# An encoder block with two attentions on one core: the decision flag made ahead of the stage change, query units from split operands, and the sums of heads turned by two DMAs

## The chip, the core and the metric

The kernel runs on one core of one Trainium2 chip. The metric is the device time of one execution in microseconds (us). The kernel before takes 1455.71 us, the median of three runs (1455.01 to 1456.9).

## What is computed

One block routes a context into a state (a small cross attention and gates, with layer norms); the next, with which this change deals, is a transformer layer on 2048 rows of width 256 with 16 heads of 16 features, whose second attention looks at the 1601 rows of the context. Cut to what matters:

```python
h = _layernorm(x, ln1_g, ln1_b)
x = x + _mha(h, h, sa_wq, ...)          # self attention, 2048 keys
h = _layernorm(x, ln2_g, ln2_b)
x = x + _mha(h, context, ca_wq, ...)    # cross attention, 1601 keys
h = _layernorm(x, ln3_g, ln3_b)
x = x + gelu(h @ mlp_w1.T + mlp_b1) @ mlp_w2.T + mlp_b2

def _mha(...):
    scores = einsum('bhqd,bhkd->bhqk', q, k) * HD ** (-0.5)
    p = softmax(scores, axis=-1)
    o = einsum('bhqk,bhkd->bhqd', p, v)
    return o.reshape(b, -1, WIDTH) @ wo.T + bo
```

All of it is float32. Where the kernel wants a product at TensorE's faster float32r rate with float32 accuracy, it splits both operands into a high and a low part and makes three products.

## The kernel before, in words

**Stages.** The first 425 us (the routed context, and keys, queries and values of the self attention) are not touched. Then come four chunks of 512 query rows of self attention (stage a = 0), four chunks of cross attention (a = 1), and an end of some 47 us.

**A chunk** works through four groups of four heads, each over all key tiles of 128 keys: 16 tiles in the self stage (64 steps a chunk) and 13 in the cross stage (52 steps). In a step PE makes the scores of the four heads in two halves (`scores`, L1457), ACT takes the exponential of each half (L1008, one instruction over 1024 columns), and PE multiplies the step before by the values (`pv`, L1474), into PSUM bank 6, where a group's sum over keys builds up. PE may be three halves of scores ahead of ACT (`LOOK`).

**Heads and sums.** After a group's last `pv`, DVE copies bank 6 (`copy_heads`, L2139). PE's first `pv` of the next group waits for this copy (semaphore `heads`, L1470). Features and softmax sums of a head stand in alternating blocks of 16 partitions, so after every second group DVE gathers the features of both in ONF and the sums in SUMS. The sums have to move by 16 partitions to stand beside the features they divide. Before, PE does this: DVE splits SUMS into RECH and SUML (L2157, L2158), PE multiplies both by a permutation matrix into bank 7 (L1496, L1497), DVE copies that to REC (L2167), takes the reciprocal in two halves (L2174) and multiplies ONF (L2178, semaphore `normed`).

**Side work.** The remaining work of a chunk of rows is laid into the steps of the next chunk by tables: `REST`, `LAST_REST` and `divide_unit` in `events` say at which step which piece stands. PE, DVE and others walk the same table in the same order, each taking its own part, so the tables are the program order of both. Pieces: `y`, the output projection of 128 rows (4 a chunk; it waits for `normed`); `h`, the turned layer norm (2); `u`, the query projection for the cross stage (2 units); `n`, norms of the queries; `m` and `o`, the MLP (8 and 4, cross stage only). They share PSUM bank 7: each piece of PE waits until DVE has taken the one before (`bank7_taken`). The list of parts gives a step for each, so "u": [25, 28, 38, 41] is two units in two parts each.

**The flag.** Whether scores are bounded (then no exact maximum is needed) is decided on data: DVE and PE reduce the norms to one number (`decide`, L1379, L2093, L2094), each engine loads it and branches (`general`). For the first three cross chunks it is made after the last self chunk, between the stages. SP waits for PE's `decided` before it loads the last group's keys of the cross stage.

**SP's queue** issues nearly all loads, in program order, each after a wait: queries of the next chunk a group at a time when `scores` of that group are done (L555, L561); during the last self chunk the cross stage's keys (L598, after the scores of each group), queries and values (L605, after `pv` of groups 1 and 3); then W1 and W2 of the MLP (L665, L666). The lines on which the order hangs:

```python
for g in range(GROUPS):
    last = (CHUNKS - 1) * GROUPS * NKS[0] + (g + 1) * NKS[0]
    sp.wait_ge(A[0]["scores"], 2 * last)
    if g == GROUPS - 1:
        sp.wait_ge(A[1]["decided"], 1)
```

Of the kernel before, what the change touches and what calls it, by code (L numbers as in the profile page):

```python
# [65 lines left out]
PARTS_OF = {"y": 1, "h": 1, "u": 2, "n": 2, "m": 2, "o": 4, "flag": 1, "w1": 1}  # L66
REST = [
# [5 lines left out]
LAST_REST = {"y": [5, 7, 9, 11], "h": [16, 17], "u": [19, 19, 21, 21], "n": [30, 30], "flag": [36], "w1": [42, 45]}  # L73
HAT_STEP = (16, 13)
GELU_STEP = 36
LOOK = 3

# [54 lines left out]
def build(nc, ctx, d, out):  # L132
# [9 lines left out]
    spreadR = m.new("spreadR", [P, P], F32)  # L142
# [35 lines left out]
    assert (TILES - LT) * HEADS * 32 * 4 >= HID * 4 + CHUNK * 4  # L178
    HCH = [m.put("HCH0", [P, CHUNK], F32, oV + LT * HEADS * 32 * 4 + HID * 4), m.new("HCH1", [P, CHUNK], F32)]
    HCL = m.put("HCL", [P, 2, CHUNK], F32, oXH + TPC * D * 4)  # L180
    W1L = m.put("W1L", [P, 2, HID], F32, oW1)
    RECH = m.put("RECH", [P, CHUNK], F32, oREC)
    SUML = m.put("SUML", [P, CHUNK], F32, oON + GP * CHUNK * 4)
# [6 lines left out]
    CAWQ = s.new("CAWQ", [P, 2, D], F32)  # L190
# [102 lines left out]
    def sm(o, n=1, p=P):  # L293
# [5 lines left out]
        saw_loaded w1_loaded w1_split w2_loaded v_cleared half_bias dve_chain dve_stepped  # L299
# [12 lines left out]
    only_cross = ("gelu", "mlp", "out_ready", "hc_lo")  # L312
# [117 lines left out]
    def events(a, first):  # L430
# [22 lines left out]
        if a == 1 or not first:  # L453
# [4 lines left out]
            ev[HAT_STEP[a]].append((o, "hat", 0, 0, True))  # L458
        return ev
# [9 lines left out]
    def _(sp):  # L469
# [75 lines left out]

        for a in range(2):
# [10 lines left out]
            def load_shift(c, g, s_to):  # L557
                rows = sd[a][:, g * GH:(g + 1) * GH, bass.ds(c * CHUNK, CHUNK)] \
                    .rearrange("r (j two) n -> two r j n", two=2)
                for odd in range(2):  # L560
                    sp.dma_start(QST[odd * HALF + SROW:odd * HALF + NROW, 2 * g:2 * g + 2, :], rows[odd]) \  # L561
                        .then_inc(s_to, 16)

# [19 lines left out]
            else:  # L583
# [3 lines left out]
                for g in range(GROUPS):  # L587

                    last = (CHUNKS - 1) * GROUPS * NKS[0] + (g + 1) * NKS[0]
                    sp.wait_ge(A[0]["scores"], 2 * last)  # L590
                    if g == GROUPS - 1:
# [10 lines left out]
                    if g % 2:  # L602

                        sp.wait_ge(A[0]["pv"], last)
                        sp.dma_start(V[:, 0:LT, (g - 1) * GH:(g + 1) * GH, :],  # L605
                                     vd.rearrange("p (k h e) -> p k h e", k=LT, h=HEADS)
                                     [:, :, (g - 1) * GH:(g + 1) * GH, :]).then_inc(s_vst[g // 2], 16)
# [55 lines left out]
            else:  # L663
                sp.wait_ge(A[0]["pv"], HALVES // 2)
# [4 lines left out]
                sp.dma_start(WOP[:], d["cawo"].rearrange("(g p) n -> p g n", p=P)).then_inc(A[1]["wop"], 16)  # L669
                general(2)  # L670
# [3 lines left out]
            for c in range(1, CHUNKS):  # L674
                for g in range(GROUPS):
# [3 lines left out]
                    load_shift(c, g, s_qst[a][g])  # L679

# [365 lines left out]
    def _(pe):  # L1046
# [324 lines left out]
        for a in range(2):  # L1371
# [15 lines left out]
            def general(f):  # L1387

                n_chunks = DECIDES[f][2]
                pe.wait_ge(at["flag"], decision(f)[2])  # L1390
                bounded = pe.value_load(flag[0:1, f:f + 1], min_val=0, max_val=1)
# [39 lines left out]

            decide(a)
            general(a)

            def scores(c, n, first):
# [26 lines left out]
            def pv(c, t):  # L1462
# [16 lines left out]
            def bank7_taken(c, kind, i, at=at):  # L1479

                q = c - 1
                s_, value = {"sums": (at["sums_taken"], c * GP + i // 2), "y": (at["y_taken"], q * TPC + i + 1),
# [3 lines left out]
                             "o": (at["mlp_taken"], q * TPC + i + 1),  # L1486
                             "flag": (A[1]["flag"], decision(2)[2])}[kind]
# [112 lines left out]
            if a == 0:  # L1600
                continue
# [779 lines left out]
```

## Time and profile before

| | us |
|---|---|
| median of three runs | 1455.71 (1455.01 to 1456.9) |
| the profiled execution's own time | 1458.83 |
| its span, first to last instruction | 1457.2 |
| PE / ACT / DVE busy | 1373.8 / 1086.6 / 590.9 |
| a self chunk, a cross chunk with MLP | about 123, about 128 |

How to read it: times in rows are us from the span's start unless ns is said. PE is TensorE's matmul, PEld its weight load, DVE VectorE, ACT ScalarE, POOL GpSimd, SP the queue that issues DMAs. In a timeline a row is: start, length, engine, line, operation, output <- input, count, and in brackets the idle time before it and what ended that. Matmuls overlap, so that the length of a row is a little more than the time to the start of the next piece. PEclk is TensorE's granted clock as a share of 2.4 GHz.

### The profile page before, as it was taken

The page shows a single profiled execution, that of the slowest core. Times are in us where ns is not written, and L with a number is a line of the kernel's source. Part 1 is how long each engine was busy: PE and PEld are TensorE (multiplying, and loading weights), DVE is VectorE, ACT ScalarE, POOL GpSimd, SP SyncE. Part 2 cuts the span into 40 slices and gives each one's busy share as a digit, 9 for nine tenths or more (in the row PEclk, how much of TensorE's full clock was granted, in tenths as well). Part 3 has the DMA queues.
Part 4 walks back from the last instruction along what each step waited for, and adds up shares of the span by engine and source line. Part 5 has one row for each costly group of instructions (what it writes and reads, how often), then busy time and mean ns, then how long its engine had stood idle before and what let it go on. Part 6 is the DMA issues. An engine that isn't in the chain of part 4 may idle for free.

```text
span 1457.2 us, 20715 instructions
## 1 busy us (share of the span) xinstructions
PE 1373.8 (94%) x8014; PEld 631.9 (43%) x8014; DVE 590.9 (41%) x1377; ACT 1086.6 (75%) x1357; POOL 47.5 (3%) x70
## 2 busy tenths in 40 slices
PE   7999989998779999999999999999999999999977
PEld 5667766786432223223322322332334333433437
DVE  5646676677740204313332331342441243144232
ACT  3543434455459999999999999799888788788843
POOL 2010000001010000000000000000000000000000
PEclk9999999999979999999999999999999999999998
DMA  9410001001268100000010353601000000000000
GB/s 306 164 47 1 1 0 58 1 1 53 72 164 119 31 23 13 27 27 14 12 52 14 46 107 62 158 30 37 24 12 16 23 12 12 23 15 1 5 11 15
DMA packets 35044, 66.00 MB, mean 45 GB/s; under 512 B 6202, under 2 KB 20092, under 8 KB 34204
## 3 DMA queue, kind: packets, MB, share of 16 engines
q1 hardware_dynamic: 29580, 43.24, 13.1%
q0 software_dynamic: 5360, 21.37, 4.1%
q8 instruction: 66, 1.08, 0.3%
q14 instruction: 38, 0.31, 0.1%
HBM read 42.70 MB, written 22.02 MB: 44 GB/s over the span
## 4 chain that ended last, share of the span: by engine, by line
PE 79%; ACT 10%; DVE 7%; issue 3%; DMA 0%; DVEq 0%; SPq 0%; ACTq 0%
PE PS L1474 27%; PE PS L1457 20%; ACT PX L1008 7%; PE PS L1556 2%; PE PS L1524 2%; PE PS L1244 2%; PE PS L1247 2%; PE PS L1206 2%; PE PS L1257 2%; PE PS L1207 2%; PE PS L1208 1%; PE PS L1505 1%; PE PS L1071 1%; PE PS L1539 1%; PE PS L1507 1%
## 5 line engine op out<-in xcount | busy, mean ns | idle before, releaser
L1008 ACT ACTIVATE PX<-PS 128x1024 f32<-128x1024 f32 (+1 forms) x928 | 869.9, 1108 | 99.8 <-PE PS L1457 77.5
L1474 PE MATMUL PS<-PX,V 128*32 128x512 f32 (+1 forms) x3712 | 498.8, 609 | 5.5 <-ACT PX L1008 4.0
L1457 PE MATMUL PS<-QST,stack 50*128 50x512 f32 (+1 forms) x1856 | 375.5, 467 | 12.1 <-ACT PX L1008 7.2
L1457 PEld LDWEIGHTS PS<-QST,stack 50*128 50x128 f32 (+1 forms) x1856 | 155.1, 184 | 391.4 <-ACT PX L1008 354.2
L1474 PEld LDWEIGHTS PS<-PX,V 128*32 128x32 f32 (+1 forms) x3712 | 74.0, 108 | 153.5 <-issue 130.9
L2139 DVE COPY OT<-PS 128x512 f32<-128x512 f32 x32 | 22.1, 692 | 214.1 <-PE PS L1474 213.3
L836 ACT ACTIVATE PH<-PS 128x512 fp32r<-128x512 f32 (+1 forms) x52 | 31.2, 600 | 82.8 <-PE PS L1187 73.0
L2174 DVE RECIPROCAL REC<-REC 128x256 f32<-128x256 f32 x30 | 52.6, 1753 | 1.0
L1556 PE MATMUL PS<-W,HIDT 128*128 128x256 f32 x192 | 44.6, 385 | 4.6 <-ACT HIDT L991 4.6
L854 ACT ACTIVATE TR<-PS,small 128x128 f32<-128x128 f32 x32 | 10.0, 364 | 51.2 <-PE PS L1247 51.2
L1866 DVE TENSOR_TENSOR PL<-PEXP,PH 128x512 fp32r<-128x512 f32 (+1 forms) x52 | 35.8, 689 | 28.0 <-ACT PEXP L837 27.2
L2235 DVE TENSOR_TENSOR XH<-PS,rows 128x256 f32<-128x256 f32 x12 | 5.1, 425 | 100.2 <-PE PS L1556 100.2
L2230 DVE TENSOR_SCALAR HIDT<-PS,cols 128x512 f32<-128x512 f32 x24 | 18.0, 751 | 66.7 <-PE PS L1507 66.7
L1206 PE MATMUL PS<-PH,CN 128*128 128x512 f32 (+1 forms) x104 | 44.0, 423 | 0.9 <-DVE PL L1866 0.9
L2203 DVE TENSOR_TENSOR XH<-PS,rows 128x256 f32<-128x256 f32 x28 | 11.9, 424 | 78.8 <-PE PS L1524 78.8
L1556 PEld LDWEIGHTS PS<-W,HIDT 128*128 128x128 f32 x192 | 35.2, 190 | 19.5 <-issue 14.8
L1207 PE MATMUL PS<-PH,CN 128*128 128x512 f32 (+1 forms) x104 | 42.2, 406 | 0.0
L1208 PE MATMUL PS<-PL,CN 128*128 128x512 f32 (+1 forms) x104 | 42.0, 404 | 0.0
L1757 DVE TENSOR_REDUCE small<-PS 128x1 f32<-128x512 f32 x64 | 35.1, 570 | 10.5 <-PE PS L1088 9.7
L1505 PE MATMUL PS<-HCH,W1H 128*128 128x512 f32 (+1 forms) x80 | 31.5, 394 | 3.8 <-DVE HCL L2250 3.8
L1167 PE MATMUL PS<-hF,SAW 128*128 128x512 f32 x64 | 31.6, 638 | 3.6 <-DVE small L1845 2.7
L2222 DVE TENSOR_SCALAR PARTS<-PS,cols 128x512 f32<-128x512 f32 x8 | 6.0, 751 | 67.1 <-PE PS L1539 67.1
(220 smaller groups left out, 1565.7 us busy)
## 6 DMA issues: line engine op xcount, KB each, us to landing
QST<-q_parts SPq DMA_DIRECT2D x192, 64.0 KB
q_parts<-PARTS POOLq DMA_DIRECT2D x16, 512.0 KB, 3.6
stack<-k_parts SPq DMA_DIRECT2D x24, 200.1 KB, 6.8
stack<-k_parts SPq DMA_DIRECT2D x18, 256.0 KB
k_parts<-KPARTS POOLq DMA_DIRECT2D x8, 512.0 KB, 3.2
v_cross<-V POOLq DMA_DIRECT2D x1, 3328.0 KB, 12.1
V<-v_cross SPq DMA_DIRECT2D x2, 1664.0 KB, 13.3
k_parts<-PARTS POOLq DMA_DIRECT2D x6, 512.0 KB, 3.3
```

The lines of the kernel that those rows point to most:

```text
L1008: act.activation(exp_place(a, h)[0:kr, :, :], PS[0:kr, slot:slot + 2, :], ACT.Exp, scale=SCALE).then_inc(at["exp"], 1)
L1167: ins = pe.matmul(PS[:, bank, :], SAW[:, "qk".index(kind), c, mm * P:(mm + 1) * P], hF[:, c, at:at + w], start=(c == 0), stop=(c == 1))
L1206: pe.matmul(PS[0:w, bank, :], c_hi, hi, start=first, stop=False)
L1207: pe.matmul(PS[0:w, bank, :], c_lo, hi, start=False, stop=False)
L1208: ins = pe.matmul(PS[0:w, bank, :], c_hi, lo, start=False, stop=last)
L1457: ins = pe.matmul(PS[0:kr, score_slot(a, h) + jj, :], KST[a][lo:lo + NROW, pair, kt * P:kt * P + kr].bitcast(F32R), QST[lo:lo + NROW, pair ...
L1474: ins = pe.matmul(PS[32 * j:32 * j + 32, 6, :], V[0:kr, kt, 2 * (g // 2 * GH + j) + g % 2, :], exp_place(a, 2 * (c * steps + t) + j // 2)[ ...
L1505: pe.matmul(out_, hi, h_hi, start=(c == 0), stop=False)
L1556: ins = pe.matmul(PS[:, 7, 0:D], HIDT[:, k, i * P:(i + 1) * P], W2[:, k, :], start=(k == 0), stop=(k == HID // P - 1))
L1757: ve.tensor_reduce(sm(MXP + tt * len(pcs) + p), PS[:, max_bank(m), 0:pcs[p][1]], AX, ALU.max) \
L1866: ve.tensor_tensor(PL[0:kr, n % RING, :].bitcast(F32R), PEXP[0:kr, n % RING, :], PH[0:kr, n % RING, :], ALU.subtract).then_inc(S["l0_lo"], 1)
L2174: ch(ve.reciprocal(part, part))
```

## The change

**Flag.** `decide(1)` becomes a piece at step 59 of the last self chunk, PE loads the flag at step 61, and the last `pv` of the self stage moves behind the first scores of the cross stage.

**Query units.** The activations HC (both stages) and the weights CAWQ (once, piece `wq` at step 20 of the first self chunk) are split; a unit is then six float32r products made in one step in place of four float32 instructions (a part of two in each of two steps). Steps of `y`, `u` and `n` change.

**Sums.** PE's two products, the split and the copy are gone. SP issues two DMAs (`turn_sums`) that bring SUMS, shifted by 16 partitions up and down, into REC and OT, and DVE puts the two together under masks (two instructions), at step 4 after the copy of the group instead of 2. The last pair of all keeps a product. In `copy_heads` the instruction on ONF now stands before the one on SUMS. The loads of values for groups 2 and 3 stand behind the cross stage's `general`.

```diff
-    {"y": [5, 8, 11, 14], "h": [19, 22], "u": [25, 28, 38, 41], "n": [54, 57]},
-    {"y": [5, 7, 9, 11], "h": [17, 18], "m": ...
+    {"y": [8, 10, 12, 14], "h": [19, 22], "u": [27, 27, 40, 40], "n": [54, 54]},
+    {"y": [8, 9, 10, 11], "h": [17, 18], "m": ...
-LAST_REST = {"y": [5, 7, 9, 11], "h": [16, 17], "u": [19, 19, 21, 21], "n": [30, 30], ...
+LAST_REST = {"y": [8, 9, 10, 11], "h": [16, 17], "u": [20, 20, 22, 22], "n": [30, 30], ...
+FIRST_REST = {"wq": [20]}
+FLAG_STEP, FLAG_LOAD = 59, 61
...
             if g % 2 == 0:
-                ev[t + 2].append((o, "sums", g, 0, True))
-                ev[t + 3].append((o, "divide", g, 0, False))
-                ev[t + 4].append((o, "divide", g, 1, True))
+                ev[t + 4].append((o, "sums", g, 0, True))
+                ev[t + 4].append((o, "divide", g, 0, False))
+                ev[t + 5].append((o, "divide", g, 1, True))
...
+        def turn_sums(a, u):
+            sp.wait_ge(A[a]["paired"], u)
+            sp.dma_start(REC[0:P - HD, :], SUMS[HD:P, :]).then_inc(A[a]["sums"], 16)
+            sp.dma_start(OT[HD:P, 1, :], SUMS[0:P - HD, :]).then_inc(A[a]["sums"], 16)
...
                     sp.wait_ge(A[0]["scores"], 2 * last)
+                    if g == GP:
+                        turn_sums(0, CHUNKS * GP - 1)
                     if g == GROUPS - 1:
                         sp.wait_ge(A[1]["decided"], 1)
...
-                    if g % 2:
...
+                    if g == 1:
+                        load_values(g, last)
...
             else:
-                sp.wait_ge(A[0]["pv"], HALVES // 2)
+                load_values(GROUPS - 1, HALVES // 2)
+                turn_sums(0, CHUNKS * GP)
                 sp.dma_start(W1[:], ...)
...
                     load_q(c, g, s_qst[a][g])
                     load_shift(c, g, s_qst[a][g])
+                    if g == GROUPS - 1:
+                        turn_sums(a, c * GP)
+                    if g == 1 and (a == 0 or c > 1):
+                        turn_sums(a, (c - 1) * GP + 1)
...
-                pe.matmul(PS[:, 7, :], spreadR[:].bitcast(F32R), RECH[:].bitcast(F32R), start=True, stop=False)
-                pe.matmul(PS[:, 7, :], spreadR[:].bitcast(F32R), SUML[:].bitcast(F32R), start=False, stop=True)
...
             def sums(c, g, at=at):
                 u = c * GP + g // 2
-                ve.wait_ge(at["sums"], u)
-                ve.tensor_copy(REC[:], PS[:, 7, :]).then_inc(at["sums_taken"], 1)
+                ve.wait_ge(at["sums"], 32 * u)
+                ch(ve.tensor_scalar(REC[:], REC[:], cols[:, LOWER:LOWER + 1], None, ALU.mult))
+                ch(ve.scalar_tensor_tensor(out=REC[:], in0=OT[:, 1, :], scalar=cols[:, UPPER:UPPER + 1], in1=REC[:],
+                                           op0=ALU.mult, op1=ALU.add))
```

**Order on the engines.** SP in the last self chunk, from the cross keys of group 1 to those of group 2. Before:

```order
L598 DMA stack<-k_parts 16x2x1601 [waits self_scores]
L598 DMA stack<-k_parts 16x2x1601 x5
L555 DMA QST<-q_parts 16x2x512 x6
L561 DMA QST<-shift 2x2x512 x2
L605 DMA V<-v_cross 128x13x256 [waits self_pv]
L598 DMA stack<-k_parts 16x2x1601 [waits self_scores]
L598 DMA stack<-k_parts 16x2x1601 x5
```

and with the change, where `REC<-SUMS` and `OT<-SUMS` are the two turning DMAs:

```order
L622 DMA stack<-k_parts 16x2x1601 [waits self_scores]
L622 DMA stack<-k_parts 16x2x1601 x5
L570 DMA QST<-q_parts 16x2x512 x6
L576 DMA QST<-shift 2x2x512 x2
L582 DMA V<-v_cross 128x13x256 [waits self_pv]
L558 DMA REC<-SUMS 112x512 [waits self_paired,self_scores]
L559 DMA OT<-SUMS 112x512
L622 DMA stack<-k_parts 16x2x1601 x6
```

The turn of the pair that DVE gathers at step 32 now stands behind the wait for the scores of group 2, ahead of its keys.

DVE in the same chunk, from that pair to the copy of group 2's heads (`COPY OT<-PS`), for which PE's next group waits. Before:

```order
L2157 CAST RECH<-SUMS 128x512 [waits dve_chain]
L2158 TENSOR_TENSOR SUML<-SUMS,RECH 128x512 [waits dve_chain]
L2160 SCALAR_TENSOR_TENSOR ONF<-OT,cols,ONF 128x512
L2167 COPY REC<-PS 128x512 [waits self_sums,dve_chain]
L2174 RECIPROCAL REC<-REC 128x256 [waits self_sums_taken]
L2174 RECIPROCAL REC<-REC 128x256 [waits dve_chain]
L2178 TENSOR_TENSOR ONF<-ONF,REC 128x512 [waits dve_chain]
L2222 TENSOR_SCALAR PARTS<-PS,cols 128x512 [waits parts_stored1,self_unit,self_normed]
L1696 TENSOR_TENSOR SQ<-PARTS 128x512 [waits self_unit_taken]
L1698 CAST PARTS<-PARTS 128x512 [waits squares]
L1699 TENSOR_TENSOR PARTS<-PARTS 128x512 [waits dve_chain]
L2139 COPY OT<-PS 128x512 [waits self_pv,parts_ready]
```

with the change:

```order
L2173 COPY OT<-PS 128x512 [waits self_pv,parts_ready]
L2184 SCALAR_TENSOR_TENSOR ONF<-OT,cols,ONF 128x512 [waits self_heads]
L2186 SCALAR_TENSOR_TENSOR SUMS<-OT,cols,SUMS 128x512 [waits dve_chain]
L2193 TENSOR_SCALAR REC<-REC,cols 128x512 [waits self_sums]
L2194 SCALAR_TENSOR_TENSOR REC<-OT,cols,REC 128x512 [waits dve_chain]
L2201 RECIPROCAL REC<-REC 128x256 [waits dve_chain] x2
L2205 TENSOR_TENSOR ONF<-ONF,REC 128x512 [waits dve_chain]
L2254 TENSOR_SCALAR PARTS<-PS,cols 128x512 [waits parts_stored1,self_unit,self_normed]
L1730 TENSOR_TENSOR SQ<-PARTS 128x512 [waits self_unit_taken]
L1732 CAST PARTS<-PARTS 128x512 [waits squares]
L1733 TENSOR_TENSOR PARTS<-PARTS 128x512 [waits dve_chain]
L2173 COPY OT<-PS 128x512 [waits self_pv,parts_ready]
```

The split and the copy from PSUM are gone; in their place two instructions on REC wait for `self_sums`, and behind them still stand the division, the query piece (`PARTS`, SQ) and the copy.

SP at the stage change. Before, from the last keys on:

```order
L598 DMA stack<-k_parts 16x2x1601 [waits cross_decided,self_scores]
L598 DMA stack<-k_parts 16x2x1601 x5
L555 DMA QST<-q_parts 16x2x512 x6
L561 DMA QST<-shift 2x2x512 x2
L605 DMA V<-v_cross 128x13x256 [waits self_pv]
L613 TENSOR_LOAD flag [waits cross_flag]
```

and with the change (the branch that is skipped left out):

```order
L622 DMA stack<-k_parts 16x2x1601 [waits cross_decided,self_scores]
L622 DMA stack<-k_parts 16x2x1601 x5
L570 DMA QST<-q_parts 16x2x512 x6
L576 DMA QST<-shift 2x2x512 x2
L633 TENSOR_LOAD flag [waits cross_flag]
...
L582 DMA V<-v_cross 128x13x256 [waits self_pv]
L558 DMA REC<-SUMS 112x512 [waits self_paired]
L559 DMA OT<-SUMS 112x512
L686 DMA W_70<-in_w1T 128x2x1024
L687 DMA W_71<-in_w2T 128x8x256
```

The values have moved behind the flag's load, and the turn of the last self pair stands behind them.

## Rows read from the trace of the kernel before

**Rows 1.** Stretches: length; busy PE, PEld, DVE, ACT, POOL; PEclk, DMA share, GB/s
```profile
548.00:671.00 123.00, 120.87 (x810) 36.78 (x806) 37.61 (x71) 118.31 (x128) 2.00 (x3) 1.00 0.08 24
1154.00:1282.00 128.00, 123.89 (x766) 49.10 (x766) 42.45 (x80) 106.38 (x110) 2.17 (x4) 1.00 0.06 18
```
**Rows 2.** Timeline of ACT, second self chunk: runs of exponentials and the idle time between
```profile
563.85 5.60 ACT L1008 ACTIVATE PX<-PS 128x1024 f32<-128x1024 f32 x6 [0.43 <-PE PS L1457]
569.89 5.61 ACT L1008 ACTIVATE PX<-PS 128x1024 f32<-128x1024 f32 x6 [0.43 <-PE PS L1457]
...
628.10 40.44 ACT L1008 ACTIVATE PX<-PS 128x1024 f32<-128x1024 f32 x44 [0.43 <-PE PS L1457]
```
**Rows 3.** Timeline of PE, same chunk: two steps with no piece between, and a query part
```profile
585.71 1.06 PE L1474 MATMUL PS<-PX,V 128*32 128x512 f32 x8
...
587.37 1.06 PE L1474 MATMUL PS<-PX,V 128*32 128x512 f32 x8
...
595.59 1.12 PE L1539 MATMUL PS<-HC,CAWQ 128*128 128x512 f32 x2
```
**Rows 4.** Timeline of PE, second cross chunk: an MLP unit of six products, then the sums' products
```profile
1084.02 0.50 PE L1505 MATMUL PS<-HCH,W1H 128*128 128x512 f32 x1
...
1085.61 0.74 PE L1457 MATMUL PS<-QST,stack 50*128 50x512 f32 x4
...
1087.27 0.51 PE L1496 MATMUL PS<-RECH,spreadR 128*128 128x512 f32 x1
...
1087.93 0.73 PE L1457 MATMUL PS<-QST,stack 50*128 50x512 f32 x4
```
**Rows 5.** Timeline of DVE, last self chunk: gathering, division, query piece, copy of the heads
```profile
856.80 0.75 DVE L2151 SCALAR_TENSOR_TENSOR SUMS<-OT,cols,SUMS 128x512 f32<-128x512 f32 x1
...
861.13 3.54 DVE L2174 RECIPROCAL REC<-REC 128x256 f32<-128x256 f32 x2
...
874.18 0.75 DVE L2222 TENSOR_SCALAR PARTS<-PS,cols 128x512 f32<-128x512 f32 x1 [8.78 <-PE PS L1539]
...
876.15 0.69 DVE L1699 TENSOR_TENSOR PARTS<-PARTS 128x512 fp32r<-128x512 f32 x1
...
886.42 0.69 DVE L2139 COPY OT<-PS 128x512 f32<-128x512 f32 x1 [9.58 <-PE PS L1474]
887.15 0.49 DVE L2148 TENSOR_SCALAR ONF<-OT,cols 128x512 f32<-128x512 f32 x1
```
**Rows 6.** Timeline of SP, last self chunk: keys of group 2
```profile
883.09 2.65 SPq L598 DMA_DIRECT2D stack<-k_parts  x6
```
**Rows 7.** DMA issues, 905 to 950 us (KB each, median us from issue to landing)
```profile
V<-v_cross SPq DMA_DIRECT2D x1, 1664.0 KB, 12.7
...
WOP<-in_cawo SPq DMA_DIRECT2D x1, 256.0 KB, 2.8
shift<-Rp POOLq DMA_DIRECT2D x1, 64.0 KB, 2.2
```
**Rows 8.** Timeline at the stage change: last self `pv` but one, SP's loads, first output projection
```profile
912.32 1.07 PE L1474 MATMUL PS<-PX,V 128*32 128x512 f32 x8
...
916.94 3.73 SPq L598 DMA_DIRECT2D stack<-k_parts  x6
...
924.13 0.54 SPq L605 DMA_DIRECT2D V<-v_cross  x1
...
930.68 1.13 PE L1524 MATMUL PS<-WOP,ONF 128*128 128x256 f32 x4
```
**Rows 9.** Busy time by stretches around both starts of a stage (columns as in rows 1)
```profile
431.00:432.00 1.00, 1.00 (x6) 0.20 (x8) 0.00 (x0) 1.00 (x2) 0.00 (x0) 0.50 1.05 123
...
923.00:924.00 1.00, 1.00 (x8) 0.23 (x10) 0.00 (x0) 1.00 (x2) 0.00 (x0) 0.57 1.11 135
...
930.00:935.00 5.00, 5.00 (x36) 1.59 (x28) 2.02 (x5) 4.38 (x6) 0.00 (x0) 1.00 1.10 341
```
**Rows 10.** Timeline at the end: the last product of the sums
```profile
1410.64 1.12 PE L1494 MATMUL PS<-SUMS,spread 128*128 128x512 f32 x2 [1.70 <-DVE SUMS L2151]
```

More of the change, by code:

```diff
@@ L458, in events @@
             ev[HAT_STEP[a]].append((o, "hat", 0, 0, True))
+        else:
+            for kind, at in FIRST_REST.items():
+                for t in at:
+                    ev[t].append((0, kind, 0, 0, True))
+        if a == 0 and c == CHUNKS - 1:
+            ev[FLAG_STEP].append((0, "flag", 0, 0, True))
         return ev
@@ L1430, in general, with scores @@
                     pe.sem_inc(at["decided"], 1)
-            decide(a)
-            general(a)
-            def scores(c, n, first):
+            if a == 0:
+                decide(0)
+                general(0, load_flag(0))
+            else:
+                general(1, bounded)
+            def scores(c, n, first, a=a, at=at, NK=NK, steps=steps):
                 h = c * steps * 2 + n
@@ L1492, in sums, with hidden @@
                 pe.wait_ge(at["paired"], c * GP + g // 2)
[L1493 to L1500 removed]
+                pe.matmul(PS[:, 7, :], spread[:], SUMS[:], start=True, stop=True).then_inc(at["sums_taken"], 1)
+            def hidden(kind, out_, i, c, span):
                 w = slice(i * P, (i + 1) * P)
[L1503 removed]
+                if kind == "u":
+                    hi, lo = CAWQH[:, c, w].bitcast(F32R), CAWQL[:, c, w].bitcast(F32R)
+                else:
+                    hi, lo = W1H[c][:, w].bitcast(F32R), W1L[:, c, w].bitcast(F32R)
                 h_hi, h_lo = HCH[c][:, span].bitcast(F32R), HCL[:, c, span].bitcast(F32R)
@@ L1533, in piece @@
                     ins.then_inc(at["hT"], 1)
-                if kind == "u":
-                    if first:
-                        pe.wait_ge(at["hc"], 2 * q + 2)
-                    for c in share(2):
-                        ins = pe.matmul(PS[:, 7, :], CAWQ[:, c, i * P:(i + 1) * P], HC[:, c, :],
-                                        start=(c == 0), stop=(c == 1))
-                    if last:
-                        ins.then_inc(at["unit"], 1)
-                if kind == "m":
+                if kind in "um":
+                    if kind == "u" and i == 0 and first:
+                        pe.wait_ge(S["wq_split"], 1)
                     if first:
@@ L1575, in chunk @@
                     for o, kind, i, part, last in ev[t]:
-                        if kind in ("copy", "divide", "hat", "w1"):
+                        if kind in ("copy", "sums", "divide", "hat", "w1", "wq"):
                             continue
@@ L1582, in chunk @@
                         held = (co, kind, i, A[o])
-                        if kind == "sums":
-                            sums(co, i, A[o])
-                        elif kind == "flag":
-                            decide(2)
+                        if kind == "flag":
+                            decide(2 if a == 1 else 1)
                         else:
@@ L2140, in copy_heads @@
                 ve.wait_ge(at["heads"], u + 1)
-                end = at is A[1] and c == CHUNKS
                 if g % 2:
```

130 lines of the change are left out of this document (66 added, 64 removed), and 2 rows, old and new, of the table REST.

## The prediction

> **What bounds the kernel now.** I read the stretches by stage first, then the timelines of ACT and PE inside a chunk, then DVE and SP around the places where the change puts a wait. In a self chunk ACT is busy for 118.3 of 123 us, in a cross chunk with MLP for 106.4 of 128 while PE has 123.9 [rows 1]. So self chunks go at ACT's pace and cross chunks at PE's. ACT makes 44 exponentials in 40.44 us, 0.916 us each if I leave out about 0.1 us of overlap at the end [rows 2]: a step of two takes 1.83 us. PE, when it is behind, starts its `pv` of one step at 585.71 and of the next at 587.37 [rows 3]: 1.66 us. PE's slack is thus 0.17 us a step, and a piece of side work is paid for by what it is longer than the slack gathered. Two output projections three steps apart show it: ACT's runs restart at 563.85 and 569.89, 6.04 us apart [rows 2], and 3 x 1.66 + 1.06 is 6.04. A projection part costs PE 1.06 us. With a full lead, ACT idles 0.43 us beside the overlap of 0.1 for such a part [rows 2], so the lead hides about 0.55 us of one piece.
>
> **The change part by part.** The sum is made against the profiled execution (span 1457.2, own time 1458.83), which is 3.1 us above the median of 1455.71; I add the difference to the median.
>
> *Sums without products.* A pair costs PE 0.66 us (1087.27 to 1087.93 [rows 4]). In self chunks (0.66 against a lead of 0.55) and at step 2 of cross chunks this stands in steps that go at ACT's pace, and is hidden: 0. The second pair of a cross chunk stands among MLP units, where PE is always behind: 0.66 in each of three chunks, **-2.0**; some 0.3 in the first cross chunk.
>
> *Query units.* Before, a unit is two parts, each as long in the queue as a projection part (records of 1.12 and 1.13 us [rows 3, 8]): 2.12 us. Six float32r products take 1.59 us (1084.02 to 1085.61 [rows 4]). PE saves 0.53 a unit, but in self chunks two parts use the lead twice and one piece once: 2 x (1.06 - 0.55) is 1.02, 1.59 - 0.55 is 1.04. So 0 in self chunks, and 2 x 0.53, **-1.1**, in the first cross chunk, where both parts of a unit already stood in one step. The split of HC gives DVE about 2.3 us a chunk (two casts, two subtractions), in 123 us of which it is busy for 38 [rows 1], ahead of a unit five steps later: 0.
>
> *Projections two steps apart or side by side.* In a self chunk the four are behind ACT by 4 x 1.06 - 6 x 0.17 - 0.55 = 2.7 us in place of about 2.5; in a cross chunk four parts take PE 10.9 us from step 8, and from step 5 to 11 they took it as long as it will now take ACT to reach step 8 and PE to do the rest. 0, with 1 us either way for all chunks.
>
> *The turned sums in an ordinary chunk.* From the copy of the heads to `paired` DVE takes 0.69 + 2 x 0.75 us [rows 5]; two DMAs and 2.2 to 2.8 us to land [rows 7] follow, then on DVE 0.49 + 0.75 for the two instructions, 3.54 for the reciprocals, 0.69 for the product [rows 5], 5.5 in all. That is some 11.5 us after the copy, and `y` stands at step 8, 14.6 us after: hidden by 3 us. SP's query loads ahead of it end before `paired`.
>
> *The turned sums in the last self chunk.* Here they aren't hidden. DVE gathers the pair at step 32 (856.80 [rows 5]) and wants it turned at step 36. But SP issues this turn only after the scores of group 2, where it issues keys at 883.09 before [rows 6]. Queued on DVE behind `self_sums`: 5.5 us of division, the second query piece with 2.56 (0.75 + 0.69 + 0.43 + 0.69, 874.18 to 876.84 [rows 5]), and then the copy of group 2's heads, without which PE can't begin `pv` of group 3. With 0.45 for two issues (2.65 for six [rows 6]) and 2.8 us to land as WOP, the row nearest in size (256 KB, against 224 each [rows 7]), the copy starts at 883.09 + 0.45 + 2.8 + 8.2 = 894.5 in place of 886.42 [rows 5]. PE and ACT stand still for **+8.0**. Bounds: 2.2 us to land gives 7.4, 4 us gives 9.2.
>
> *TensorE's clock after it.* At the stage change PE's work ends at 913.4 but for a last `pv`, the flag holds it up, and the clock is at 1.2 GHz until about 923.9 [rows 8, 9]; SP's load shows that PE got on at 916.9, so it was low for nearly 7 us of work. After the wait at the first stage's start it was still low at 431 to 432 [rows 9], some 7 us after its first scores. At half clock a step takes 3.32 us in place of 1.83, so 6.7 us cost 3.0: **+2.9**. Bounds: 0 if the clock stays, 3.6 if it is low for 8 us. The Trainium skill ("TensorE: Matmul & The Clock Gate", Terms) takes the penalty as the throttled time times (1 - K/N), at half clock half of it; by that the term would be 3.4 and the sum 0.5 more.
>
> *The stage change.* SP's loads of the last keys wait for `decided`, which comes at 916.94 now [rows 8], and with the flag made earlier when the last but one `pv` is through, at 912.32 + 1.07 = 913.4: 3.5 us sooner. Without anything else PE would come to step 8 at about 931 (the last exponential ends near 914.1, a `pv` of 1.07, eight steps of 1.83, and up to a microsecond for refilling the lead). But `y` waits for the last self pair, and its turn is queued on SP behind keys, queries and 1664 KB of values. Before, the values landed at 924.13 + 12.7 = 936.8 [rows 7, 8], 19.9 us after the first key load; now at 933.4. The turned 448 KB need 1.3 us at 341 GB/s [rows 9] and DVE 5.6: `y` starts at 940.4 instead of 930.68 [rows 8]. Then four parts in four steps and one more to step 13: 940.4 + 4 x 1.06 + 5 x 1.66 = 952.9, before 930.68 + 4 x 1.06 + 8 x 1.66 = 948.2. **+4.7**; without the wait it would be 931 + 4.24 + 8.3 = 943.5, a saving of 4.7. PE has stood for 9 us, and is behind here, so low clock costs half of 6.7: **+3.3** (0 to 4). Values landing a microsecond later, as after their first load's issue, give 5.7.
>
> *Small ones.* At the end DVE now does ONF ahead of SUMS, 0.75 us more ahead of the last product, for which PE waits 1.70 [rows 10]: **+0.8**. Flag matmuls and load inside the last chunk: +0.2.
>
> **Sum:** 8.0 + 2.9 + 4.7 + 3.3 + 0.8 + 0.2 - 2.0 - 0.3 - 1.1 = **+16.5**, so 1472.2 us. Its own bounds, in the same order and with 1 us for ordinary chunks: low 7.4 + 0 + 4.7 + 0 + 1.0 - 3.4 - 1.0 = +8.7, high 9.2 + 3.6 + 5.7 + 4.0 + 1.0 - 3.4 + 1.0 = +21.1: 1464 to 1477.
>
> **The rivals.**
> 1. *The last turn doesn't queue behind the values.* Then it lands soon after `paired`, `y` doesn't wait, and the stage change gives its 4.7: 8.0 + 2.9 - 4.7 - 2.4 (the small terms and savings together) = +3.8, 1459.5. The Trainium skill ("DMA: Bandwidth & Descriptors", Queues, rings and completion order) says that completion isn't first in, first out for one issuing engine; by this rule the order of issue promises nothing. The trace speaks for order in this queue: 924.13 plus 12.7 is long after the small transfers that need 2.2 to 2.8 [rows 7, 8], so the values themselves stood behind keys. 9%.
> 2. *Faster: both turns come in time.* One mechanism: DVE isn't held up, because the turned sums arrive within the steps left for them, at step 36 of the last self chunk and at step 4 of the first cross chunk. Price: no stall, no low clock, -4.7 - 2.4 = -7.1, 1448.6. It decides if the two stalls together stay under 7 us. Against it stands the order: a wait for the scores of group 2 can't end before step 46, ten steps after DVE wants the sums. 8%.
> 3. *Freed PE time shows in self chunks too*, products and units in full: 6 x 0.66 + 6 x 0.53 = 7.1 less, 1465. Against: ACT's share [rows 1]. 6%.
> 4. *The turned sums are late in every chunk*, behind the query loads, by 3 us beyond the margin: six chunks, +18, 1490. Against: 3 us of margin. 4%.
>
> **How the numbers follow.** The forecast has 73%. About 0.2%, 2.9 us, is what a measurement can tell from no change. The range reaches from rival 1's upper part over 3 and the forecast to somewhat above its own end: 1460 to 1480; faster, rival 4 and half of rival 1 lie outside, some 17%. Faster 0.08; within 0.2% 0.05 (rival 1, a little better than its number); slower 0.87.
>
> **What would show each step.** In the last self chunk DVE's first instruction on REC after step 32 waits for a DMA until about 886, and PE and ACT have a gap of 8 us near 887, after which PEclk is 0.5 for some us. At the stage change PE goes from self to cross scores within about a microsecond, SP's last key load starts 3.5 us after the last scores' issue or sooner, and PE has a second gap of 9 us ahead of the first L1524 group, ended by DVE's ONF, itself after a DMA that lands after the values. Self chunks 2 and 3 stay within 1 us of 123, cross chunks drop by 0.7. I am wrong if either gap is missing, if the turned sums land before the values, or if ordinary self chunks change by more than 1 us.

## The result and the profile after

The changed kernel takes 1474.03 us (median of four runs, 1471.87 to 1481.1) beside 1455.93 for the kernel before on the same chip: ratio 1.0132, 95% interval 1.0112 to 1.0152. It is slower by 1.3%, some 18 us; 1472.2 was predicted, from a sum of +16.5. Its profiled execution took 1471.87 us, with a span of 1470.2.

The page (engines' busy time; then DVE's first instruction on the turned sums, with its idle time and what ended that):

```profile
PE 1366.5 (93%) x8000; PEld 633.1 (43%) x8000; DVE 594.1 (40%) x1380; ACT 1083.6 (74%) x1357; POOL 47.4 (3%) x70
...
L2193 DVE TENSOR_SCALAR REC<-REC,cols 128x512 f32<-128x512 f32 x15 | 7.3, 487 | 85.3 <-DMA OT<-SUMS 85.2
```

PE's work fell by 7.3 us and ACT's by 3.0, yet the kernel is slower, so the loss is in waits. DVE waits 85 us for turned sums in all, which costs nothing where it has nothing else to do. The same views as in [rows 1], for a self and a cross chunk:

```profile
544.00:667.00 123.00, 121.09 (x810) 37.98 (x806) 39.11 (x72) 118.03 (x129) 1.99 (x3) 1.00 0.11 31
1165.00:1293.00 128.00, 124.33 (x772) 49.01 (x770) 40.88 (x76) 106.65 (x110) 2.44 (x5) 1.00 0.09 26
```

Ordinary self chunks are as they were, and an ordinary cross chunk is 0.7 us shorter. **Where the time went** is seen from one instruction that stands in both programs at the same steps: DVE's copy of the heads (`COPY OT<-PS`, L2139 before, L2173 now, 32 of them). The time between two copies' starts, in us:

| stretch | before | changed | difference |
|---|---|---|---|
| start to the first copy | 457.93 | 453.81 | -4.12 |
| from there to step 32 of the last self chunk | 398.14 | 398.03 | -0.11 |
| last self chunk, step 32 to 48 | 30.35 | 40.16 | +9.81 |
| its step 48 to cross step 0 | 30.16 | 30.84 | +0.68 |
| cross step 0 to 13 | 31.77 | 43.24 | +11.47 |
| rest of the first cross chunk | 75.84 | 75.09 | -0.75 |
| three cross chunks, up to the last copy | 384.92 | 380.36 | -4.56 |
| last copy to the end | 48.09 | 48.67 | +0.58 |

The first row is work that the change doesn't touch (but for one cast of a constant on DVE, which is gone), and so are 2.6 of the -4.56: two stretches in which the kernel before shows a lower clock and the changed one doesn't.

The kernel before:

```profile
80.00:100.00 20.00, 17.65 (x72) 12.14 (x70) 10.43 (x49) 6.96 (x16) 2.99 (x3) 0.83 0.07 24
1026.00:1030.00 4.00, 4.00 (x22) 0.85 (x20) 1.48 (x3) 3.38 (x4) 0.00 (x0) 0.57 0.01 4
```

The changed kernel:

```profile
80.00:100.00 20.00, 17.65 (x83) 12.20 (x82) 11.80 (x50) 7.56 (x17) 2.98 (x3) 1.00 0.07 24
```

Over all traces of this study the first copy lies between 453.8 and 459.0 us, and such a dip (1.3 us for a stretch of about 28.4) comes in some programs and not in others that share the code. The last row scatters too: in programs that share the changed kernel's end it is 48.6 to 50.2 us. All this is scatter, and I leave the first row and the 2.6 us out below: they are why the spans differ by only 13.0 us. Without them the rows add up to +19.7.

**The first wait**, last self chunk. SP, DVE and PE of the changed kernel (beside [rows 5, 6]):

```profile
878.81 0.55 SPq L558 DMA_DIRECT2D REC<-SUMS  x1
879.40 0.60 SPq L559 DMA_DIRECT2D OT<-SUMS  x1
880.04 2.94 SPq L622 DMA_DIRECT2D stack<-k_parts  x6
```
```profile
883.70 0.49 DVE L2193 TENSOR_SCALAR REC<-REC,cols 128x512 f32<-128x512 f32 x1 [29.59 <-DMA OT<-SUMS]
...
892.00 0.69 DVE L2173 COPY OT<-PS 128x512 f32<-128x512 f32 x1
```
```profile
892.84 1.94 PE L1508 MATMUL PS<-PX,V 128*32 128x512 f32 x8 [9.99 <-DVE OT L2173]
895.86 1.93 PE L1508 MATMUL PS<-PX,V 128*32 128x512 f32 x8
898.87 1.09 PE L1508 MATMUL PS<-PX,V 128*32 128x512 f32 x8
```

DVE stands for 29.6 us at the turned sums, the copy of the next heads is behind it, and PE stands for 10.0 us. Then two steps go at 3.01 us, with the granted clock at 0.50 (1.2 GHz). **The second wait**, at the stage change (beside [rows 8]):

```profile
920.43 3.64 SPq L622 DMA_DIRECT2D stack<-k_parts  x6
924.11 2.75 SPq L570 DMA_DIRECT2D QST<-q_parts  x6
926.90 0.58 SPq L576 DMA_DIRECT2D QST<-shift  x2
934.31 0.61 SPq L582 DMA_DIRECT2D V<-v_cross  x1
934.98 0.97 SPq L558 DMA_DIRECT2D REC<-SUMS  x1
```
```profile
921.70 1.07 PE L1508 MATMUL PS<-PX,V 128*32 128x512 f32 x8 [0.32 <-ACT PX L1036]
...
950.25 2.08 PE L1558 MATMUL PS<-WOP,ONF 128*128 128x256 f32 x4 [11.60 <-DVE ONF L2205]
```
```profile
944.62 0.49 DVE L2193 TENSOR_SCALAR REC<-REC,cols 128x512 f32<-128x512 f32 x1 [19.52 <-DMA OT<-SUMS]
```

PE goes from one stage to the other with short waits for ACT only (0.3 us here and 0.7 us at 924.32), and then waits 11.6 us for the turned sums, for which DVE stands 19.5 us. The landings there (columns as in [rows 7]) and the clock in the stretches after the two waits:

```profile
V<-v_cross SPq DMA_DIRECT2D x1, 1664.0 KB, 8.5
...
REC<-SUMS SPq DMA_DIRECT2D x1, 224.0 KB, 8.2
OT<-SUMS SPq DMA_DIRECT2D x1, 224.0 KB, 8.6
```
```profile
894.00:896.00 2.00, 2.00 (x12) 0.65 (x12) 0.00 (x0) 0.46 (x1) 0.00 (x0) 0.50 0.68 258
...
950.00:955.00 5.00, 4.75 (x16) 1.87 (x16) 1.65 (x5) 1.02 (x1) 0.00 (x0) 0.50 0.00 0
```

At the end, in place of 1.70 us [rows 10]:

```profile
1423.85 1.34 PE L1529 MATMUL PS<-SUMS,spread 128*128 128x512 f32 x2 [2.49 <-DVE SUMS L2186]
```

### The profile page after: what moved, and what is told of

Its sections match the earlier page's. It is cut to its first block, busy times and chain, and to the rows that moved or that the text cites. A ratio compares the mean times of both kernels' runs of the same rounds, so it can differ in the third digit from the quotient of the medians.

```text
span 1470.2 us, 20699 instructions
## 1 busy us (share of the span) xinstructions
PE 1366.5 (93%) x8000; PEld 633.1 (43%) x8000; DVE 594.1 (40%) x1380; ACT 1083.6 (74%) x1357; POOL 47.4 (3%) x70
## 4 chain that ended last, share of the span: by engine, by line
PE 72%; ACT 13%; DVE 8%; issue 4%; DMA 2%; SPq 1%; DVEq 0%; PEld 0%; PEldq 0%; ACTq 0%
PE PS L1508 24%; PE PS L1491 17%; ACT PX L1036 10%; PE PS L1583 2%; PE PS L1558 2%; PE PS L1272 2%; PE PS L1275 2%; PE PS L1539 2%; PE PS L1285 2%; PE PS L1234 2%; PE PS L1235 1%; PE PS L1236 1%; PE PS L1541 1%; PE PS L1540 1%; PE PS L1685 1%
## 5 line engine op out<-in xcount | busy, mean ns | idle before, releaser
L1491 PE MATMUL PS<-QST,stack 50*128 50x512 f32 (+1 forms) x1856 | 386.2, 474 | 10.2 <-ACT PX L1036 7.7
L1491 PEld LDWEIGHTS PS<-QST,stack 50*128 50x128 f32 (+1 forms) x1856 | 158.9, 183 | 410.5 <-ACT PX L1036 377.6
L2173 DVE COPY OT<-PS 128x512 f32<-128x512 f32 x32 | 22.1, 692 | 226.2 <-PE PS L1508 226.2
L1558 PE MATMUL PS<-WOP,ONF 128*128 128x256 f32 x112 | 33.4, 423 | 11.6 <-DVE ONF L2205 11.6
L1583 PEld LDWEIGHTS PS<-W,HIDT 128*128 128x128 f32 x192 | 35.2, 190 | 19.4 <-issue 14.8
L2193 DVE TENSOR_SCALAR REC<-REC,cols 128x512 f32<-128x512 f32 x15 | 7.3, 487 | 85.3 <-DMA OT<-SUMS 85.2
L1558 PEld LDWEIGHTS PS<-WOP,ONF 128*128 128x128 f32 x112 | 20.0, 198 | 37.7 <-issue 23.5
```

The source lines that it names most:

```text
L1491: ins = pe.matmul(PS[0:kr, score_slot(a, h) + jj, :], KST[a][lo:lo + NROW, pair, kt * P:kt * P + kr].bitcast(F32R), QST[lo:lo + NROW, pair ...
L1558: ins = pe.matmul(PS[:, 7, 0:D], ONF[:, g, i * P:(i + 1) * P], WOP[:, g, :], start=(g == 0), stop=(g == GP - 1))
L1583: ins = pe.matmul(PS[:, 7, 0:D], HIDT[:, k, i * P:(i + 1) * P], W2[:, k, :], start=(k == 0), stop=(k == HID // P - 1))
```

## The experiments

All are edits of the changed kernel, timed against the kernel before in runs on the same chip; its median was 1457.59 us for e1 to e4, 1455.50 for e5 to e8 and 1455.37 for e9 to e11. "Turn 7" is the turn of the pair gathered at step 32 of the last self chunk, "turn 8" that of the last self pair. Stretches are again those between DVE's copies: A is step 32 to 48 of the last self chunk, B step 48 to cross step 0, C cross step 0 to 13.

| | median | ratio to before | A | B | C |
|---|---|---|---|---|---|
| before | 1455.93 | 1 | 30.35 | 30.16 | 31.77 |
| changed | 1474.03 | 1.0132 (1.0112 to 1.0152) | 40.16 | 30.84 | 43.24 |
| e1 | 1463.89 | 1.0048 (1.0032 to 1.0065) | 30.29 | 28.84 | 43.17 |
| e2 | 1469.42 | 1.0096 (1.0069 to 1.0122) | 40.07 | 29.70 | 36.35 |
| e3 | 1468.27 | 1.0075 (1.0057 to 1.0094) | 40.32 | 30.81 | 33.28 |
| e4 | 1471.93 | 1.0108 (1.0087 to 1.0129) | 40.09 | 29.69 | 39.75 |
| e5 | 1454.91 | 0.9997 (0.9984 to 1.0010) | 30.30 | 28.84 | 33.23 |
| e6 | 1454.80 | 0.9994 (0.9981 to 1.0007) | 30.30 | 30.15 | 32.12 |
| e7 | 1451.29 | 0.9969 (0.9956 to 0.9981) | 29.70 | 28.84 | 33.61 |
| e8 | 1449.20 | 0.9956 (0.9943 to 0.9968) | 30.28 | 28.84 | 28.43 |
| e9 | 1448.70 | 0.9949 (0.9931 to 0.9968) | 30.29 | 28.84 | 28.42 |
| e10 | 1447.75 | 0.9951 (0.9936 to 0.9966) | 29.70 | 28.84 | 28.44 |
| e11 | 1454.84 | 0.9993 (0.9982 to 1.0003) | 30.30 | 30.16 | 31.74 |

**e1, turn 7 early.**

```diff
-                    if g == GP:
-                        turn_sums(0, CHUNKS * GP - 1)
...
                     if g == 1:
+                        turn_sums(0, CHUNKS * GP - 1)
                         load_values(g, last)
```

> The turn of the pair gathered at step 32 of the last self chunk goes ahead of the values of groups 0 and 1, where SP has only waited for the scores of group 1. My theory (the 8 us stall of that chunk is this turn's place in SP's queue, and the half clock after it is a consequence of the stall): the interval from the copy at step 32 to that at step 48 goes from 40.16 back to 30.3 us, the next from 30.84 to 28.9, together -11.8: 1462.2. Rival A (DVE's queue is too full there in any case, with two query pieces and the division): less than 2 us won, 1472 or more. Rival B (the half clock after the stall has another cause): -9.8, 1464.2, and the granted clock near 895 is still 0.5.

A fell by 9.87 and B by 2.00: the theory to 0.1 us, both rivals out. The copy waits for PE again, not for DVE's own queue:

```profile
856.49 0.54 SPq L558 DMA_DIRECT2D REC<-SUMS  x1
```
```profile
865.55 0.49 DVE L2192 TENSOR_SCALAR REC<-REC,cols 128x512 f32<-128x512 f32 x1 [9.68 <-DMA OT<-SUMS]
...
883.90 0.69 DVE L2172 COPY OT<-PS 128x512 f32<-128x512 f32 x1 [10.07 <-PE PS L1507]
```

Even here the turn took 8.5 us to land, with the keys and queries of group 1 issued just ahead of it; only the place in the program makes that harmless. The clock that stood at 0.50 after the wait is now whole:

```profile
894.00:896.00 2.00, 2.00 (x18) 0.48 (x14) 0.56 (x1) 2.00 (x4) 0.00 (x0) 1.00 0.00 0
```

**e2, turn 8 ahead of the values.**

```diff
-                load_values(GROUPS - 1, HALVES // 2)
                 turn_sums(0, CHUNKS * GP)
+                load_values(GROUPS - 1, HALVES // 2)
```

> At the stage change the last self pair's turn and the values of groups 2 and 3 change places in SP's queue, both still behind the flag's load. My theory (transfers of this queue land in the order in which they are issued): the turn is issued near 934.3 and lands 3 us later, as in ordinary chunks, so that DVE starts at about 938 in place of 944.6 and the first output projection at about 943.7 in place of 950.25: -6.5, 1467.5. Rival (order of issue promises nothing; the turned sums are late because they share the engines with 1664 KB of values and 2 MB of MLP weights): they land near 943 again, less than 1.5 us won, 1472.5 or more.

C fell by 6.89. The turned sums landed 2.8 and 3.5 us after their issue in place of 8.2 and 8.6:

```profile
REC<-SUMS SPq DMA_DIRECT2D x1, 224.0 KB, 2.8
OT<-SUMS SPq DMA_DIRECT2D x1, 224.0 KB, 3.5
```

So in this queue the place behind 1664 KB of values costs some 5 us. 6.2 us of waiting for PE remained, since the turn is still behind the flag's load:

```profile
945.34 2.08 PE L1558 MATMUL PS<-WOP,ONF 128*128 128x256 f32 x4 [6.22 <-DVE ONF L2205]
```

**e3, turn 8 on GpSimd.** (DVE waits for `last_turned` for this pair.)

```diff
-                turn_sums(0, CHUNKS * GP)
...
+        with gp.Fori(0, CHUNKS - 1) as c:
+            store_queries(c)
+        gp.wait_ge(A[0]["paired"], CHUNKS * GP)
+        gp.dma_start(REC[0:P - HD, :], SUMS[HD:P, :]).then_inc(S["last_turned"], 16)
+        gp.dma_start(OT[HD:P, 1, :], SUMS[0:P - HD, :]).then_inc(S["last_turned"], 16)
+        store_queries(CHUNKS - 1)
```

> The same turn is issued by GpSimd, on a queue of its own, as soon as the pair is gathered (near 924.5). My theory: it doesn't stand behind SP's keys, queries, flag load and values, lands by about 930, and the output projection at step 8 isn't held up (PE comes there at 938.6): the 11.6 us of waiting go, and about 1.5 us of half clock after it: 1461. Rival (the transfer is slow because the DMA engines are full, whichever queue it has): it lands near 936, the projection starts near 942: -8, 1466. Rival (the half clock at the stage change has another cause than the wait): -11.6 without the clock, 1462.4.

My theory fell, and the first rival was nearer: C gained 9.96, and the wait shrank to 3.2 us but didn't go. The DMAs were issued at once, on a queue of their own, and took three times as long as on the same queue where nothing else is loaded (e9):

```profile
REC<-SUMS POOLq DMA_DIRECT2D x1, 224.0 KB, 9.1
OT<-SUMS POOLq DMA_DIRECT2D x1, 224.0 KB, 10.2
```
```profile
947.05 1.13 PE L1565 MATMUL PS<-WOP,ONF 128*128 128x256 f32 x4 [3.19 <-DVE ONF L2215]
```
```profile
931.00:936.00 5.00, 5.00 (x39) 1.54 (x36) 0.00 (x0) 5.00 (x7) 0.71 (x2) 1.00 0.98 120
```

The DMA engines are busy (0.98) at only 120 GB/s: these are the last group's keys, whose issue began 5 us ahead of the turn, and its queries, issued at the same time as the turn. Here a queue of its own didn't help against engines that were full.

**e4, values back ahead of the flag's load.**

```diff
+                    if g == GROUPS - 1:
+                        load_values(g, HALVES // 2)
...
-                load_values(GROUPS - 1, HALVES // 2)
                 turn_sums(0, CHUNKS * GP)
```

> The values of groups 2 and 3 go back ahead of the flag's load and branch, as before the change; the turn stays behind both. SP took 6.8 us from its last query load to the values in the changed kernel, and three packets of the instruction queues are recorded there between 932 and 935, just when the data queue has run empty. Theory 1 (SP's next code is fetched there, and the fetch stands behind the data that were queued): with 1664 KB more queued the fetch takes longer, the turn is issued at 938 or later and the first projection starts at 948 to 951: within 2 us of the change, 1472 to 1476. Theory 2 (the pause has a fixed length): the turn is issued at 935, the values have landed by then, first projection at about 945: -5, 1469. Theory 3 (no fetch falls there in this program, as before the change): the turn is issued at 930 and lands behind the values near 938: -6.5, 1467.5.

Between theories 1 and 2: the first projection started at 948.90 (theory 1), C fell by 3.49. SP's pause at the load and branch grew:

```profile
928.19 0.58 SPq L582 DMA_DIRECT2D V<-v_cross  x1
937.80 0.58 SPq L558 DMA_DIRECT2D REC<-SUMS  x1
```

It is 9.0 us from the end of the first row to the second with the values queued, against 6.8 without. It ended before the values had landed (13.5 us after their issue), so it didn't wait for all that was queued. The traces of the other programs have the same pause: 6.6 to 7.8 us in the seven where only keys and queries are on their way, 8.0 to 9.2 us in the four where the turned sums are on their way too, on GpSimd's queue (e3, e5, e6, e7). So it is no fixed length and seems to depend on what is queued, but it differs by 1.2 us between programs with the same loads queued. That the cause is the fetch of SP's next code is not shown. For it speaks that three packets of the instruction queues start around the end of the pause in the changed kernel (932.3 to 934.9), and that in the kernel before, where SP was through at 926.25, none starts between 918 and 932.

**e5, both moves** (the edits of e1 and e3).

> Both moves at once: the turn at step 32 ahead of the values of groups 0 and 1, the last self pair's turn on GpSimd. If the two stalls are separate, as my theory has it, their gains add: 11.9 us (two intervals of DVE's copies in the last self chunk) and 10.0 us (the interval from cross step 0 to 13) less than the change, 1452, which is 0.3% under the kernel before. Rival (one stall shortens the other, since the keys of the last group are queued by the clock and not by PE's progress): together 17 us or less, 1457, no gain on the kernel before.

In the trace the gains add: A -9.86, B -2.00, C -10.01, 21.9 us. The timed ratio went from 1.0132 to 0.9997, some 20 us. The version equals the kernel before; it is not the 0.3% faster that I expected.

**e6, flag between the stages**: `decide(1)` and the load before `general(1)`, the last self `pv` ahead of them, no piece for the flag in the last self chunk.

> As e5_both_moved, but the flag is made and loaded between the stages, as in the kernel before, and the last self pv stands before it. Theory from the trace of before: the early flag is worth 4.7 us, so this one is 4.7 slower, 1457. Rival: with the flag late, SP issues the last group's keys later than GpSimd issues the turn, the turned sums land in 3 us in place of 10, and the 3.2 us for which the projection still waits go: net 1.5 slower, 1453.5. If the flag is worth nothing: 1449.

No difference (B + C 62.27 against 62.07), as neither number said. The reason I gave for the rival was wrong: SP's first keys were issued 2 us ahead of the turned DMAs, not behind them, and these took 6.1 and 10.6 us to land. What hid the wait is that PE came later. The flag let ACT stand still for 3.5 us, before the turn was issued, and the steps after that ran at a lower granted clock (0.59 on average from 914 to 922). PE was ready for the projection 16.6 us after the turn's first issue, in e5 after some 13, and so it waited 0.2 us for it and not 3.2. One delay covered the other.

**e7, units in two parts.**

```diff
-    {"y": [8, 10, 12, 14], "h": [19, 22], "u": [27, 27, 40, 40], "n": [54, 54]},
+    {"y": [8, 10, 12, 14], "h": [19, 22], "u": [27, 30, 38, 41], "n": [54, 54]},
```

> As e5_both_moved, with each query unit of self chunks in two parts of three products three steps apart (steps 27, 30, 38, 41) in place of six in one step. The changed kernel's trace has 0.87 us of idle ACT for each whole unit; a part of 0.8 us should show no more than 0.8 - 0.55 = 0.25. Two whole units cost 1.74 us a chunk, four parts 1.0: -0.7 in each of three self chunks, 2.2 in all, 1450. Rival (PE makes up for the lead by other pieces, so ACT's idle time only moves): within 0.5 us of e5_both_moved.

The stretch with the units fell from 30.29 to 29.70 in each of three self chunks, 1.8 us where 2.2 was expected. ACT's idle time at a unit, changed kernel and then e7:

```profile
597.24 23.94 ACT L1036 ACTIVATE PX<-PS 128x1024 f32<-128x1024 f32 x26 [0.87 <-PE PS L1491]
```
```profile
598.28 5.61 ACT L1042 ACTIVATE PX<-PS 128x1024 f32<-128x1024 f32 x6 [0.18 <-PE PS L1497]
604.15 14.77 ACT L1042 ACTIVATE PX<-PS 128x1024 f32<-128x1024 f32 x16 [0.26 <-PE PS L1497]
```

The medians of e5 and e7 differ by 3.6; only 1.8 of it is in these stretches. The rest has no cause shown: the two profiled executions differ by 0.2 us, since e5's lies 2.9 under its median.

**e8, turn 8 ahead of the last keys** (on SP, behind the wait for `decided`).

> The turn at step 32 early, and the last self pair's turn on SP ahead of the last group's keys, so that it is issued when nothing is queued (SP waits for the pair, 4 to 5 us later than it would issue those keys). This order is only for the branch that this data takes. My theory (whatever is issued behind those keys and queries waits some 14 us for them, on any queue and the code fetch too): the turned sums land within 3 us of their issue, near 928, DVE is done by 934, and the projection at step 8 doesn't wait at all; against the GpSimd version 3.2 us of waiting and about 1.5 of half clock go: 1447.5. Keys and values come 5 us later and are needed only at steps 39 and 26. Rival (PE has other work missing there, and the clock falls anyway): 1450 to 1452.

As my theory had it: C 28.43, no wait of PE before the projection. The turned sums landed after 2.8 and 4.2 us, on SP's own queue.

**e9, keys held back**: the signal `decided`, for which SP waits before the last group's keys, is given by PE at step 4 of the first cross chunk.

```diff
-                if f == 1:
-                    pe.sem_inc(at["decided"], 1)
...
+                    if a == 1 and first and t == 4:
+                        pe.sem_inc(at["decided"], 1)
```

> As e5_both_moved (early turn at step 32, last self pair's turn on GpSimd), but PE lets SP begin the last group's keys only at step 4 of the first cross chunk, some 7 us later, so that the turn has the DMA engines for itself; unlike e8 this order holds in both branches of the flag. My theory (the turn was slow on GpSimd's queue only because 1.2 MB of keys in small packets were ahead of it): turned sums land within 3 to 4 us of their issue, no wait before the first output projection, from the last self chunk's step 48 to cross step 13 it takes 57.3 us as in e8 in place of 62.1: 1449.5, 0.4% under the kernel before. Rival (a transfer on GpSimd's queue takes 6 us or more by itself): some 59 us for that stretch, 1451.5.

The same stretches as e8, to 0.02 us. The turn on GpSimd's queue lands like one on SP's when the keys aren't ahead of it, and PE goes from `pv` to the first projection without a wait (second view):

```profile
REC<-SUMS POOLq DMA_DIRECT2D x1, 224.0 KB, 2.6
OT<-SUMS POOLq DMA_DIRECT2D x1, 224.0 KB, 3.2
```
```profile
930.00 1.06 PE L1511 MATMUL PS<-PX,V 128*32 128x512 f32 x8
930.99 1.13 PE L1561 MATMUL PS<-WOP,ONF 128*128 128x256 f32 x4
```

**e10, all gains.** Beside the `u` steps of e7, the last copy's order:

```diff
+                    end = at is A[1] and c == CHUNKS
+                    if end:
+                        ve.scalar_tensor_tensor(out=SUMS[:], ...).then_inc(at["paired"], 1)
                     ch(ve.scalar_tensor_tensor(out=pair, ...))
...
```

> As e9_keys_held_back, with query units of self chunks in two parts each (0.6 us in each of three self chunks in the trace of e7), and the sums ahead of the features for the very last copy alone, where PE waits for them (the changed kernel takes 0.6 us longer than the kernel before from its last copy to the end): 1.8 + 0.6 = 2.4 less than e9, 1447. Rival (one of the two doesn't add up): 1448.5.

A is 29.70 as in e7, and PE's wait for the last sums is back at 1.70 from 2.49, but the timed gain over e9 can't be told (0.9951 against 0.9949, intervals of 0.3%). In the traces the last three cross chunks take 382.10 us in e10 and 380.35 in e9, which share this code; such dips of the clock hide most of the gain there.

**e11, flag between the stages, nothing to cover it** (e9 with the edit of e6).

> As e9_keys_held_back, but the flag is made and loaded between the stages. In e6 this cost nothing, where the projection waited for the turned sums in one program and PE for the flag in the other. My theory (the early flag is worth what I read from the trace of before, and e6 didn't show it only because a wait of 3.2 us took its place): here nothing covers it, and the program is 4.7 us slower than e9, with PE's clock at 1.2 GHz for some 7 us after the pause: 1454. Rival (the early flag is worth little): within 1.5 us of e9.

B + C is 61.90 against 57.26: 4.64 us. The medians differ by 6.1; the other 1.5 is not explained. The granted clock after the pause, and in e9 over the same time:

```profile
914.00:922.00 8.00, 7.29 (x32) 2.05 (x32) 3.84 (x6) 5.71 (x6) 1.11 (x2) 0.57 0.20 60
```
```profile
914.00:922.00 8.00, 7.22 (x50) 2.21 (x50) 2.60 (x4) 7.33 (x9) 1.11 (x2) 1.00 0.18 57
```

## Why the prediction was right, and where its terms were off

The mechanism and both places were right; e1 takes the first wait away and e9 both, and A, B and C go with them. Term by term:

- **Stall of the last self chunk, +8.0: 9.8.** Above my upper bound of 9.2. What is queued on DVE behind the sums was right (8.30 us from its first instruction to the copy, 8.2 predicted). The error is in the transfer: from the first issue to DVE 4.9 us in place of 0.45 + 2.8, because the second issue began 0.6 us after the first and its DMA landed 4.3 us after that, with keys issued right behind. In ordinary chunks, with nothing behind it, the same DMA lands after 2.9 to 3.1 us. I had the price of one issue from a group of six, where each is cheaper.
- **Clock after it, +2.9: 2.0**, shown by e1. A step took 3.01 us at half clock, not 3.32: I had doubled PE's 1.66, and it isn't doubled in full. The trace of before has it already (`pv` at 920.67 and at 923.68, at the stage change). Beside ACT's 1.83 two such steps lose 2.4. e2 and e4 have the same stall and lose only 0.9: there the granted clock is back at 1.00 some 4 us after the copy of the heads, in the changed kernel 7 us after it. So this term scatters. The Trainium skill ("TensorE: Matmul & The Clock Gate", Terms) would make it half of the throttled time, 3.0 us for the 6 us from 892.8 to 898.9; the trace is below this.
- **Stage change, +4.7 + 3.3 = 8.0: about 10.2.** A wait plus low clock of 12.7, less a saving of 4.7, was the forecast. Against e9, the changed kernel has 74.08 us for B + C, 16.8 more, of which 2.0 belong to the first stall; 14.8 are left, 11.6 of it PE's wait and 3.2 a rest that I put down to the clock (3.3 forecast). The wait was 9.4 by the forecast. I let the values follow the queries as closely as before and overlooked what it costs that in the new order SP's load and branch stand ahead of them: 6.8 us from the end of the last query load to the values, where SP, before the change, went through them in 1.6 us, between the values and W1. The values landed 22.4 us after the first key load, not 19.9.
- **The saving of the early flag, 4.7: 4.64** (e11 against e9).
- **Small terms.** End: the wait grew by 0.79 (0.8 forecast); the +0.58 of the whole stretch is less than its scatter. Cross products: -0.7 in each of three chunks as forecast (37.07 to 36.38). First cross chunk: -0.75 in place of -1.4. Self chunks 0, as forecast. The 2.5 us by which the four projections of a self chunk were said to be behind ACT before comes out as 2.2 by the prediction's own prices; the term was put at 0, and stays there.

Of the **rivals**, the first (the turn isn't held up behind the values) rested on a rule of the Trainium skill ("DMA: Bandwidth & Descriptors", Queues, rings and completion order), that completion isn't ordered by issue. In the changed kernel the trace fits the forecast's order: the values landed at 942.8, the two turning DMAs at 943.2 and 944.6, and in e2 the turn lands 5 us sooner after its issue with two lines exchanged. But the order isn't strict: in e4 the first turning DMA, issued 9.6 us after the values, landed at 941.1 and the values at 941.7. And e3 and e9 say that order in one queue was only part of it: on another queue the turn took 10.2 us behind the keys and 3.2 without them. I had put all of the wait down to the place in SP's queue. Of its 11.6 us, 3.2 are left when the turn is issued at once and only the keys are ahead (e3), and 5.4 go when it changes places with the values (11.6 to 6.2, e2). That leaves 3.0 for its late issue behind the flag's load, by difference only. The second rival, the faster one, gave 1448.6 us if both turns came in time. e9 is this case, made on purpose, and measured 1448.70. The third fell (self chunks unchanged), as did the fourth.

The agreement of the total is better than that of its terms: the stall and the stage change cost 1.8 and 2.2 us more, and the clock after the stall 0.9 less. The rows of the traces add up to +19.7, the medians differ by 18.1, and the interval leaves 16.3 to 22.1 open; that 16.5 came so close to 18.1 is in part luck. That the spans differ by only 13.0 us comes from where these two executions lie: the profiled one of before is 2.9 above its median, the other 2.2 below.

## What to carry to other kernels

When an engine's work is handed to a DMA, the cost is where the DMA is issued in a queue that has waits of its own, what the receiving engine has queued behind it, and what the DMA engines are moving at that time; the instruction counts say none of it. Here three changes of place (one turn a group earlier, one on another queue, a large load held back by four steps) turned +1.3% into -0.5%. And two waits side by side hide what either part is worth: the flag's 4.6 us couldn't be seen until the other wait was gone.

## What was not expected of the hardware

- 448 KB between two tiles on the chip land 3.2 us after the second issue when the engines are free (e9). They took 8.5 to 10.6 us when 1.2 MB of keys and 0.4 MB of queries were issued next to them, from 6 us before to 3 us after, on the same queue (e1) or another (e3, e5, e6). Those keep the engines 0.98 busy at 120 GB/s (e3), where 341 GB/s are moved while the values land [rows 9].
- SP's load of the flag and its branch took 6.8 us behind queued loads, 9.0 us with 1664 KB more queued (e4), and 1.6 us in the kernel before, with keys, queries and values queued there too. Over all programs with the new order it was 6.6 to 9.2 us.
- Runs of one program scatter by up to 0.7% (e6: 1447.86 us at a mean granted clock of 0.982, 1458.17 at 0.975), and the traces show dips of the granted clock in stretches that no edit touches.
